# The second attention pass: one stream over two sets, three probability tiles, and a band cut by GpSimd in some sets

## What is computed

```python
    qkv = x @ Wqkv + bqkv
    q, k, v = jnp.split(qkv, 3, axis=-1)
...
    scores = jnp.einsum('bhid,bhjd->bhij', q, k) * scale
    idx = jnp.arange(n)
    band = jnp.abs(idx[:, None] - idx[None, :]) <= HALF
    neg = jnp.asarray(jnp.finfo(scores.dtype).min, scores.dtype)
    scores = jnp.where(band[None, None], scores, neg)
    attn = jax.nn.softmax(scores, axis=-1)
    out = jnp.einsum('bhij,bhjd->bhid', attn, v)
    out = out.transpose(0, 2, 1, 3).reshape(b, n, d)
    return out @ Wout + bout
...
x = L0_attn_x
xn = _layernorm(x, axis=-1)
x = x + _L0_attn_ref(xn, L0_attn_Wqkv, L0_attn_bqkv, L0_attn_Wout, L0_attn_bout) + _L0_ffn_ref(xn, L0_ffn_wqkv, L0_ffn_w1, L0_ffn_w2)
xn = _layernorm(x, axis=-1)
...
```

## Time and profile before

| | |
|---|---|
| runs | 1708.3, 1714.09, 1727.36 us; median 1714.09 |
| profiled execution | 1726.19 us, of it the span of the trace 1724.1 us |
| granted TensorE clock, mean | 0.920 of full speed |
| busy in the span | PE 1327.1 us (77%), DVE 1246.4 (72%), ACT 732.6 (42%), POOL 675.8 (39%) |
| second-pass scores on PE | mask L957 512 matmuls, scores L959 1024 |

### The profile page before, as it was taken

One profiled execution on the slowest core, in us unless ns is written; L12 is line 12 of the kernel. 1 busy time (PEld: TensorE's weight loads), 2 busy tenths in 40 slices (PEclk: granted clock), 3 DMA queues, 4 the chain that ended last, 5 costly groups with the idle time before them and its releaser, 6 DMA issues.

```text
span 1724.1 us, 27415 instructions
## 1 busy us (share of the span) xinstructions
PE 1327.1 (77%) x8730; PEld 822.9 (48%) x8762; DVE 1246.4 (72%) x2289; ACT 732.6 (42%) x1007; POOL 675.8 (39%) x534
## 2 busy tenths in 40 slices
PE   3499987768888788768887888768877898745564
PEld 2266665534444576434444676424444676311223
DVE  3544455668999874569999864569999873379974
ACT  3222142437666144347655244256654334333320
POOL 5100000017989030028988130038987120046624
PEclk7699999888999999889999999889999999869997
DMA  6120011014111030013110030023110030022200
GB/s 164 51 42 1 1 31 31 13 38 123 56 44 32 2 58 16 15 57 112 54 43 25 4 56 17 14 79 95 61 41 16 4 56 17 0 63 67 62 6 13
DMA packets 54852, 72.32 MB, mean 42 GB/s; under 512 B 8396, under 2 KB 25604, under 8 KB 54660
## 3 DMA queue, kind: packets, MB, share of 16 engines
q1 hardware_dynamic: 49696, 68.40, 15.1%
q10 hardware_dynamic: 5012, 2.12, 0.5%
HBM read 61.36 MB, written 9.04 MB: 41 GB/s over the span
## 4 chain that ended last, share of the span: by engine, by line
PE 48%; DVE 27%; issue 11%; ACT 5%; POOL 3%; DMA 3%; SPq 1%; ACTq 1%; DVEq 1%; POOLq 0%; PEldq 0%
PE ps L800 11%; DVE hs L1216 8%; PE ps L813 6%; PE ps L723 3%; DVE hc L1228 3%; PE ps L957 3%; PE ps L973 3%; DVE negmax L1281 3%; PE ps L871 3%; PE ps L959 3%; PE ps L872 2%; PE ps L714 2%; DVE x L1202 2%; PE ps L1003 2%; DMA ks<-parts_d 2%
## 5 line engine op out<-in xcount | busy, mean ns | idle before, releaser
L800 PE MATMUL ps<-xnT,w1T 128*128 128x512 f32 (+1 forms) x768 | 384.4, 620 | 71.3 <-DVEq L186 42.1
L448 POOL TENSOR_TENSOR dBu<-du,bs 128x512 f32<-128x512 f32 x256 | 325.5, 1276 | 159.9 <-DMA bs<-b_d 117.2
L1216 DVE TENSOR_TENSOR_SCAN hs<-ps,carry,dBu 128x512 f32<-128x512 f32 x256 | 320.5, 1268 | 22.4 <-POOL dBu L448 18.9
L606 ACT ACTIVATE ps<-delta,A_s 128x512 f32<-128x512 f32 x256 | 173.3, 688 | 210.3 <-DVE hs L1216 209.7
L813 PEld LDWEIGHTS ps<-w2T,hT 128*128 128x128 f32 (+1 forms) x1536 | 198.2, 201 | 119.5 <-DVE x L1202 77.3
L813 PE MATMUL ps<-w2T,hT 128*128 128x128 f32 (+1 forms) x1536 | 207.3, 288 | 44.5 <-DVE x L1202 44.5
L438 POOL TENSOR_TENSOR y<-y,hc 128x512 f32<-128x512 f32 x168 | 213.4, 1271 | 23.0 <-DVE hc L1228 22.9
L800 PEld LDWEIGHTS ps<-xnT,w1T 128*128 128x128 f32 (+1 forms) x768 | 130.1, 187 | 187.8 <-issue 150.5
L1191 DVE TENSOR_TENSOR hT<-sa,ps 128x512 f32<-128x512 f32 (+1 forms) x192 | 129.8, 676 | 82.1 <-PE ps L800 61.0
L632 ACT ACTIVATE pt<-ps 128x1024 f32<-128x1024 f32 x128 | 130.0, 1022 | 114.4 <-PE ps L959 114.4
L414 POOL COPY x<-x 128x1024 f32<-128x1024 f32 x4 | 4.1, 1036 | 441.0 <-DVEq L186 441.0
(11 more groups left out here) (220 smaller groups left out, 1974.9 us busy)
## 6 DMA issues: line engine op xcount, KB each, us to landing
bs<-b_d SPq DMA_DIRECT2D x128, 256.0 KB, 3.3
qs<-parts_d SPq DMA_DIRECT2D x144, 64.0 KB
ks<-parts_d SPq DMA_DIRECT2D x144, 64.0 KB
parts_d<-part SPq DMA_DIRECT2D x8, 768.0 KB, 3.6
st<-in_L_ffn_w SPq DMA_DIRECT2D x16, 128.0 KB, 5.8
x_in<-in_L_attn_x SPq DMA_DIRECT2D x4, 512.0 KB, 4.3
out<-res SPq DMA_DIRECT2D x4, 512.0 KB, 3.2
st<-in_L_ffn_w SPq DMA_DIRECT2D x8, 176.0 KB, 6.0
```

Of the source, the lines that this page charges most:

```text
L448: pool.tensor_tensor(dBu[g][n_ % 2][:, :], du[:, g, tb * HALF:(tb + 1) * HALF], bs[n_ % RING][:, :], ALU.mult)\
L606: act.activation(decay_bank(g), delta[:, g, tb * HALF:(tb + 1) * HALF], ACT.Exp, scale=A_s[:, g, n_:n_ + 1]).then_inc(S["dA_r"], 1)
L800: pe.matmul(bank((2, 6)[k % 2] if gate else k % 2)[0:m, :], w1T[:, k // 3, gate * F + f0:gate * F + f0 + m], xnT[:, BAND + tb * HALF:BAND ...
L1216: dve.tensor_tensor_scan(hs[g][:, :], decay_bank(g), dBu[g][n_ % 2][:, :], carry[:, g, n_:n_ + 1], ALU.mult, ALU.add).then_inc(S["h_s"], 1)
```

## The change

The second passes on the two sets of a pair become one stream of 16 tiles (`second_passes`). TensorE's scores run two tiles ahead of the values' tile and the values stand one behind: scores of w + 2, then values of w - 1. pt has three tiles instead of two. In T0 for all four sets, in T1 to T3 for sets 2 and 3 (`cut_by_pool`), the mask matmul is left out; the exponential then is taken of all 256 keys, and GpSimd writes zeroes outside the band into pt (`cut_band`, two affine selects a tile), and the values wait for GpSimd (cut_r) instead of ScalarE. Sets 0 and 1 of T1 to T3 keep the mask. In T1 to T3 GpSimd does the requantising first, then the cuts of sets 2 and 3.

```diff
+        def cut_by_pool(b1, s):
+            return b1 is None or s >= 2
+        def cut_count(b0, b1, s, i):
+            if b1 is None:
+                return b0 * SETS * TILES + s * TILES + i + 1
+            return (b0 + 1) * 2 * TILES + (s - 2) * TILES + i + 1
-            pt = [sb(f"pt{i}", [P, HPS, 2, P], F32, sec) for i in range(2)]
+            pt = [sb(f"pt{i}", [P, HPS, 2, P], F32, sec) for i in range(NPT)]
+NPT = 3
-CREDIT = {"pv_p": 2, "p_r": 2, "max_r": 2, "att_r": 2, "o_c": 2, "nmT_p": 1, "nmT_r": 1, "mp_out": 1, "xqT_r": 2, "gu_p": 2, "tgg_r": 2, "q_done": 2, "hb_r": 2,
+CREDIT = {"pv_p": 3, "p_r": 2, "max_r": 2, "att_r": 2, "o_c": 2, "nmT_p": 1, "nmT_r": 1, "mp_out": 1, "xqT_r": 2, "gu_p": 2, "tgg_r": 2, "q_done": 2, "hb_r": 2,
...
             def T(b0, b1):
-                if b1 is None:
-                    return
+                if b1 is not None:
+                    requantise(b1)
+                if b0 is not None:
+                    for s in range(SETS):
+                        if cut_by_pool(b1, s):
+                            for i in range(TILES):
+                                cut_band(b0, s, i)
+            def cut_band(b0, s, i):
+                w = (b0 * SETS + s) * TILES + i
+                p = pt[(s * TILES + i) % NPT]
+                pool.wait_ge(S["p_r"], nth("p_r", w))
+                settle(pool)
+                pool.affine_select(out=p[:, :, 0, :], in_=p[:, :, 0, :], compare_op=ALU.is_ge, fill=0.0, base=0,
+                                   pattern=[[0, HPS], [-1, P]], channel_multiplier=1)
+                pool.affine_select(out=p[:, :, 1, :], in_=p[:, :, 1, :], compare_op=ALU.is_ge, fill=0.0, base=0,
+                                   pattern=[[0, HPS], [1, P]], channel_multiplier=-1).then_inc(S["cut_r"], 1)
+            def requantise(b1):
...
-                def probs(s, i, par):
+                def probs(s, i):
                     w = (b0 * SETS + s) * TILES + i
+                    par = i % 2
                     act.wait_ge(S["s2_p"], w + 1)
-                    act.wait_ge(S["pv_p"], nth("pv_p", w - 2))
-                    act.activation(pt[par][:, :, :, :], bank(2 * par, 2), ACT.Exp, scale=float(DH) ** -0.5).then_inc(S["p_r"], 1)
+                    act.wait_ge(S["pv_p"], nth("pv_p", w - NPT))
+                    act.activation(pt[(s * TILES + i) % NPT][:, :, :, :], bank(2 * par, 2), ACT.Exp, scale=float(DH) ** -0.5).then_inc(S["p_r"], 1)
...
-                    for i in range(TILES):
-                        probs(s, i, i % 2)
-                        if i == 0 and s % 2 == 0:
+                    for w in range(2 * TILES):
+                        probs(s + w // TILES, w % TILES)
+                        if w == 0:
                             minus_max(s + 1)
-                        if i == 5:
-                            gather(s, 0)
-                    gather(s, 1)
+                        if w % 4 == 1 and w > 1:
+                            gather(s + (w - 5) // TILES, (w - 5) // 4 % 2)
+                    gather(s + 1, 1)
...
-                    def scores_k(i):
-                        pe.wait_ge(S["p_r"], nth("p_r", base + i - 2))
+                    def scores_k(w):
+                        s, i = s0 + w // TILES, w % TILES
+                        if i == 0:
+                            pe.wait_ge(S["mp_in"], (b0 * SETS + s + 1) * 16)
+                        pe.wait_ge(S["p_r"], nth("p_r", (b0 * SETS + s0) * TILES + w - 2))
+                        by_pool = cut_by_pool(b1, s)
...
-                            pe.matmul(o, identb[:, :], mask_k[:, :], start=True, stop=False)
+                            if not by_pool:
+                                pe.matmul(o, identb[:, :], mask_k[:, :], start=True, stop=False)
...
-                        pe.wait_ge(S["p_r"], nth("p_r", base + i))
+                        if cut_by_pool(b1, s):
+                            pe.wait_ge(S["cut_r"], cut_count(b0, b1, s, i))
+                        else:
+                            pe.wait_ge(S["p_r"], nth("p_r", (b0 * SETS + s) * TILES + i))
...
                     scores_k(0)
-                    for i in range(TILES):
-                        if i + 1 < TILES:
-                            scores_k(i + 1)
-                        if i == 0 and s % 2 == 0:
-                            turn_max(s + 1)
-                        values(i)
+                    scores_k(1)
+                    turn_max(s0 + 1)
+                    for w in range(2 * TILES):
+                        if w + 2 < 2 * TILES:
+                            scores_k(w + 2)
+                        if w:
+                            values(w - 1)
+                    values(2 * TILES - 1)
...
-                    second_pass(s)
-                    second_pass(s + 1)
+                    second_passes(s)
```

More of the change, by code:

```diff
@@ L672, in T @@
                         minus_max(s2)
-                    second_pass(s2)
-                    second_pass(s2 + 1)
+                    second_passes(s2)
             sections(act, M, T, C)
@@ L944, in turn_max, with second_passes @@
                     t.then_inc(S["nmT_p"], 1)
-                def second_pass(s):
+                def second_passes(s0):
                     if b0 is None:
                         return
-                    base = (b0 * SETS + s) * TILES
-                    def scores_k(i):
-                        pe.wait_ge(S["p_r"], nth("p_r", base + i - 2))
+                    def scores_k(w):
[4 more added lines that the diff above has]
+                        by_pool = cut_by_pool(b1, s)
                         for h in range(HPS):
@@ L956, in scores_k, with values @@
                             q = qs[s % 2][0:K_ALL, h, i * P:(i + 1) * P]
-                            pe.matmul(o, identb[:, :], mask_k[:, :], start=True, stop=False)
+                            if not by_pool:
+                                pe.matmul(o, identb[:, :], mask_k[:, :], start=True, stop=False)
                             for j in range(2):
-                                t = pe.matmul(o[:, j * P:(j + 1) * P], ks[s % 2][0:K_ALL, h, (i + j) * P:(i + j + 1) * P], q, start=False, stop=(j == 1))
+                                t = pe.matmul(o[:, j * P:(j + 1) * P], ks[s % 2][0:K_ALL, h, (i + j) * P:(i + j + 1) * P], q,
+                                              start=by_pool, stop=by_pool or j == 1)
                         t.then_inc(S["s2_p"], 1)
-                    def values(i):
+                    def values(w):
+                        s, i = s0 + w // TILES, w % TILES
                         o = bank(4 + i // 4)
@@ L973, in values @@
                                 t = pe.matmul(o[32 * h:32 * h + DH + 1, (i % 4) * P:(i % 4 + 1) * P], vaug[:, i + j, s * HPS + h, :],
-                                              pt[i % 2][:, h, j, :], start=False, stop=(j == 1), skip_group_check=True)
+                                              pt[(s * TILES + i) % NPT][:, h, j, :], start=False, stop=(j == 1), skip_group_check=True)
                         t.then_inc(S["pv_p"], 1)
-                    pe.wait_ge(S["mp_in"], (b0 * SETS + s + 1) * 16)
-                    pe.wait_ge(S["max_r"], nth("max_r", (b0 * SETS + s // 2 * 2 + 1) * TILES + TILES - 1))
-                    if b1 is not None and s == 0:
+                    pe.wait_ge(S["max_r"], nth("max_r", (b0 * SETS + s0 + 1) * TILES + TILES - 1))
+                    if b1 is not None and s0 == 0:
                         pe.wait_ge(S["hb_r"], nth("hb_r", b1 * TILES + TILES - 1))
-                    if b1 is not None and s == 2:
+                    if b1 is not None and s0 == 2:
                         pe.wait_ge(S["hqT_r"], nth("hqT_r", b1 * TILES + TILES - 1))
@@ L1376 @@
     "std0_r", "std1_r", "xn0_r", "xn1_r", "link0", "link1", "dBu0_r", "dBu1_r", "ln0", "ln1", "q_scale",
-    "q_round", "den_r", "g_p", "a_p", "cc_p", "settled", "section", "h_s", "st_tr", "rowset",
+    "q_round", "cut_r", "den_r", "g_p", "a_p", "cc_p", "settled", "section", "h_s", "st_tr", "rowset",
     "pad", "rowdma", "stack_in", "x_in", "hi_r", "mid_r", "lo_r", "b_out", "part_out", "nmT_r", "mp_out", "mp_in", "pv_p",
```

2 lines of the change are left out of this document (1 added, 1 removed).

## The result

| | us, median (runs) | kernel before beside it | ratio, 95% interval |
|---|---|---|---|
| changed kernel | 1726.17 (20) | 1717.86 (20) | 1.005, 1.003 to 1.007 |

Half a per cent slower, where 0.85% faster was forecast, and above the top of the range (1717.0). With more runs the kernel before stands at 1717.86, 3.8 us above the median from which the sum was taken. The profiled execution of the changed kernel took 1725.53 us (span 1723.5).

A forecast was written before the change was run, and what follows sets the result against it. TensorE bounds second passes at 1.56 us a tile; transfers released by set 0's eighth values bound first pairs. Sum -20.4 - 2.0 + 6.3 + 1.5 = -14.6 us off 1714.09: 1699.5 us, range 1688 to 1717.

The forecast's parts named there:

- second pairs: Sets 2 and 3 in all four sections: each pair 23.3 us against 28.36, 5.1 earlier, 20.4 us gained.
- T0, first to second pair: T0's first pair, also cut: only the eighth values' 2.0 us count, the rest is spent waiting for set 3's stack.
- T1 to T3, first to second pair: Masked first pairs: new order starts transfers 2.1 us later, 6.3 us lost, plus 1.5 for the clock.
- the clock inside the cut passes: Rival: idle TensorE drops to half speed in cut passes, a third of 80 tiles losing 0.9 us each, 1724 us; chance 0.05.
- The cut's pace: GpSimd in cut passes: two selects of 0.61 us and one wait, 1.30 us a tile, so GpSimd sets the pace.
- the lock with VectorE: VectorE's multiply excludes GpSimd: three meetings a cut pair cost 0.7 us, at worst 2; set against overlapping instructions.
- The masks did not hide the weight loads: Rival for TensorE's cut tiles: whole loads before score matmuls, scores 0.8 us a tile, sum +3, 1717 us; chance 0.20.
- about -5 us: The sum if the skill page's 81 ns per load and matmul held, making a tile's scores 0.65 us.
- a fixed time after set 0 is done: When a section's first pair ends: set 2's transfers wait for set 0's eighth values; first pass 16.7 to 18.6 us later in T1 to T3.
- a sign of being wrong: Signs named: score tiles above 0.5 us, selects above 0.7, or first passes on set 2 starting no later.
- late transfers cost nothing: Rival: set 2's transfers end when they did before, so 6.3 us come back, 1693 us; chance 0.13.
- The clock after the longer idle time: First pass on set 2 in T1 to T3: 0.5 us a section more at the lower clock, 1.5 in all, bounds 0 and 5.

The follow-up runs named there:

- e2: Changed kernel plus, in cut pairs, five dummy matmuls before the wait for row maxima and five behind the third score tile: 1713.76 us, 0.9949 of the kernel before.
- e7: Changed kernel with both dummy-matmul fills, and set 2's and 3's transfers issued after the eighth score tile instead of the eighth values: 1698.88 us, ratio 0.9886.
- e12: Changed kernel with mask matmuls put back in the last twelve of the sixteen tiles of each cut pair, none in the first four: 1744.99 us (one run).

## Why the prediction was wrong, step by step

The stretches that change, means of two profiles each, after less before:

| step | forecast | measured |
|---|---|---|
| second pairs | -20.4 | -0.5 (114.2 - 114.8) |
| T0, first to second pair | -2.0 | +3.0 (60.1 - 57.2) |
| T1 to T3, first to second pair | +6.3, and +1.5 for the clock | +5.8 (195.1 - 189.3) |
| sum | -14.6 | +8.3 |

The ratio gives +8.6 us (0.005 x 1718). The single profiles lie far apart: the first two give -3.9, +3.8 and +0.2 us for the three rows, the second two +2.9, +2.1 and +11.6. That the sum of the means comes so near the ratio is in part luck.

- **The step that failed is the clock inside the cut passes**, priced at nothing in the sum and given 0.05 as a rival. Its argument was that TensorE "works 1.17 of 1.30 us there". That is true of the stream at its pace and says nothing of its start, where three score tiles without masks, a turn and a wait of 1.12 us follow on 1.51 us of waiting. Once low, a tile takes TensorE 1.94 us, more than GpSimd's 1.3, and the pace is lost until the clock returns. Filling the two waits gives back 17 us (e2), and the forecast's ratio, 0.9915 (1699.5 / 1714.09), lies within e2's interval. The rival's price was near, 1724 us against 1726.17, but by luck in part: it took a third of the 80 tiles at 0.9 us each; measured are 0.64 us a low tile (1.94 - 1.30) and, by an estimate from the granted clocks of the five cut pairs (67 us at the low level), about 35 tiles.
- **The cut's pace was right.** Selects of 0.64 to 0.70 us for 0.61, the lock with VectorE 0.45 us every four tiles, in all 1.3 us a tile; second pairs of 23.7 us for 23.3 where the clock holds (e2, e7): -19.8 us in e7 (95.0 against 114.8) for the forecast's -20.4.
- **The masks did not hide the weight loads.** Eight score matmuls take 0.55 us, 69 ns each. By the Trainium skill, "TensorE: Matmul & The Clock Gate", section "Back-to-back issue gap", they would take 0.65, an estimate from its figure for one; the row shows 0.55, and the measurement decides. The sum of "about -5 us" that the prediction put beside that rule did not follow from it either: 0.65 us of scores would have made TensorE's tile 1.21 us, still below GpSimd's 1.30.
- **T0's first pair.** At full clock the eighth values came 13.4 us after the start (244.54 - 231.11 in e2), forecast 12.9, before 14.67. In the changed kernel they came after 19.0 (250.00 - 230.99), at the low level. And the stacks' lengths vary by more than the 2.0 us: in e2 set 2's took 16.3 us from issue to issue (245.30 to 261.60), 13.5 before, so the full clock alone won nothing there.
- **T1 to T3.** The eighth values are 2.1 us later to a hundredth (16.96 for 14.86). That a first pair ends "a fixed time after set 0 is done" was too simple: in T1 TensorE was released by the transfer 15.4 us after the eighth values (620.31 to 635.75), 17.3 before, and in the second profile of before VectorE was the bound. In the first profiles the first pass on set 2 came no later, summed over the three, after the pair's start (32.4, 31.1 and 32.2 us in T1 to T3, before 32.2, 33.4 and 31.5), which the prediction names as a sign of being wrong and has as a rival, that late transfers cost nothing. In the second profiles it came later, 33.5, 32.6 and 34.0 us against 29.8, 30.8 and 30.9. So the size, +5.8 for +7.8, is near on the mean and no confirmation. The idle time before it, 4.76, 3.47 and 4.60 us in the first profile, is below the 6 forecast.
- **The clock after the longer idle time.** From the start of the first pass on set 2 to the second pair's start, T1 to T3 together take 95.6 us before and 97.1 after in the first profiles, 94.4 and 97.3 in the second: +1.5 and +2.9 for the +1.5 forecast. How much of it is the clock is not separated.
- **The base.** 3.8 us of the miss is the median of three runs.

Still open: what makes set 2's stack take 10.3 us from issue to issue in T1 of e2 and 16.3 in T0 (617.64 to 627.93, 245.30 to 261.60) at the same bytes; no row shown here goes with it. The first profile of before had three slow ones, and so they looked like the rule. Open, too, is why T0's second pair lost less in one profile of the changed kernel than in the other, and what in the start of a pair, the light work or the waits, lowers the clock.

## What to carry to other kernels

Before taking filler work off TensorE, look at the first few microseconds of each pass, not at its mean load: if the lighter start is followed by a wait, the clock may fall there and a good part of the pass then runs on an engine of half the speed. Filling two waits with matmuls whose result nobody reads cost nothing that shows here and returned the gain forecast for the second pairs. Profile the kernel before twice: a bound that is read from one execution may be a slow transfer of that execution.

## What the runs showed of the hardware

- The clock stood almost wholly at its lower level while TensorE was busy 17.62 of 19.01 us (granted 0.58, T0's first pair). So a busy engine is no proof of the high level. With mask matmuls among the scores from the fifth tile on, the level came back sooner in most second pairs (e12: granted 0.83 to 0.89; changed kernel 0.71 to 0.87). The Trainium skill, "TensorE: Matmul & The Clock Gate", section "HAM oscillation — how this bites in real kernels", puts the fall down to waits for DMA between bursts of matmuls; here the waits at the start are of 1.51 and 1.12 us, for VectorE and ScalarE, and no gap is left in the low rows behind them, so this case is not explained by that account.
- Matmuls of zeros held the high level: the fills multiply by zerob, and the four pairs of e2 have clock 1.00.
- An affine select of 512 elements a partition took 0.63 to 0.64 us by itself and 1.09 us beside VectorE's multiply of two inputs in SBUF (303.61; the multiply ran from 303.15 to 304.20).
